# Output projections of both attentions from float32r high and low parts, on one Trainium2 core

## The chip, the core and the metric

The kernel runs on one core of a Trainium2 chip. The core's engines are TensorE (PE in the profile; its weight loads are PEld), VectorE (DVE), ScalarE (ACT), GpSimd (POOL) and SyncE (SP), which here only issues DMAs. Each engine works through its own list of instructions in order and waits on semaphores that others raise. The metric is device time in microseconds (us), as the median of several runs.

## The reference, cut to what matters

A perceiver block on 64 sequences of 64 tokens, width 256, 16 heads of 16: cross-attention to a context of 256 tokens per sequence, causal self-attention, and a feed-forward part with ternary weights and 8-bit activations. In float32:

```
x = x + xattn(layernorm(x), ctx, ctx)    # q, k, v = projections with bias; softmax; out @ Wo.T + bo
x = x + attn(layernorm(x))               # qkv = x @ w_qkv + b; causal; y @ w_out + b_out
x = x + ffn(layernorm(x))                # silu(gate) * up, then down, all quantized
```

The change touches the two products `out @ Wo.T` and `y @ w_out`.

## The kernel before, in words

The 4096 tokens are 32 tiles of 128 (two sequences each). There are three stages, one after the other over all tiles: cross-attention (about 14 to 560 us), self-attention (to about 790 us) and feed-forward. The order of each engine's instructions is written out by hand, in functions called from a `body` (cross-attention) or `body2` (self-attention); most tiles run in hardware loops (`Fori`), some are written out. In loops a wait whose count depends on the tile number takes instructions of its own (ISA, REGISTER_ALU); in written-out tiles it does not. On VectorE the cross-attention tiles 1 to 7 and 21 to 30 are in loops, 8 to 20 written out.

A cross-attention tile t has two halves s (one sequence each), called (t,0) and (t,1). TensorE's order in `body` is: keys k(t,1), transposes of the probabilities (t,0) in four groups, output projection of the tile before (`pe_out`, L361), values v(t,1) (`pe_v`, L299), transpose of the next tile's normalized rows (`pe_xt`, L264), scores (t,1) (L315), probabilities times values (t,0), queries of t+1, reciprocals r(t,0), keys (t+1,0), transposes (t,1), values (t+1,0), scores (t+1,0), and so on. The product with the values is `o`; VectorE multiplies it with the reciprocals (L428) and adds the two heads' parts into `oT` (L431).

The keys and values are already projected from float32r parts: `ch` is the context rounded to float32r by ScalarE, `cl` the rest, computed by GpSimd (L502), and three products (high by high, high by low, low by high) stand for the float32 one. The output projection is a plain float32 product of `oT` with `wo_sb`, two contraction steps, written by TensorE as four instructions.

`xt_ps`, the target of `pe_xt`, and `y_ps`, the target of `pe_out`, are the same 256 columns of one PSUM bank. For `pe_xt(t+1)` VectorE has to have written `xn` (L387): statistics (L375, L377), `vare` (L382), GpSimd's power (`rstd`, L493), then the normalization. VectorE's order there is: o(t-1,1), statistics of t+1, k(t,1) out of PSUM (L397), the reciprocal (L421), the copy of transposed group 0 (L414), xn, y of the tile before (L438), the copy of group 2, v(t,1).

In self-attention `pe_out2` (L725) does the same product per tile, behind the projection and r2 and ahead of `pe_v2` (L659). There GpSimd makes `rm` (L841), `kbd` (L833), `rstd`, the low part of the input (L826, `xl`, which shows as cl in the rows) and adds a bias to `x_all` (L848).

Of the kernel before, what the change touches and what calls it, by code (L numbers as in the profile page):

```python
# [26 lines left out]
P = 128  # L27
# [17 lines left out]
def block_kernel(nc, x, ctx_t, wq, bq, wk, bk, wv, bv, wo, bo, w_qkv, b_qk, b_v2, w_out, b_out,  # L45
# [8 lines left out]
    with ctx:  # L54
# [22 lines left out]
        wo_sb = sb("wo_sb", [P, KT, D])  # L77
        bq_sb = sb("bq_sb", [P, KT])
# [9 lines left out]
        wout_sb = sb("wout_sb", [P, KT, D])  # L88
        bout_sb = sb("bout_sb", [P, D])
# [29 lines left out]


# [8 lines left out]
        kbd4 = [sb(f"kbd4{s}", [P, KT, 4, P]) for s in range(2)]  # L129
# [19 lines left out]
        wd_b = wb_all[:, 8:12, :].rearrange("p a (c n) -> p (a c) n", c=2)  # L149
        w_abs = sb("w_abs", [P, 12])  # L150
# [80 lines left out]
        o_ev = sem("o_ev")  # L231
        y_mm = sem("y_mm")
# [190 lines left out]
        def dve_o(v, t, s):  # L423
            b = t * 2 + s
            v.wait_ge(pv_mm, b + 1)
            v.wait_ge(r_ev, b + 1)
            v.wait_ge(o_ev, b)
            nc.vector.tensor_tensor(o_prod[:], o_ps, r_sb[:], ALU.mult).then_inc(op_done, 1)  # L428
            v.wait_ge(op_done, b + 1)

            nc.vector.tensor_tensor(oT[:, :, s * L:(s + 1) * L], o_prod[:, :, 0, :],  # L431
                                    o_prod[:, :, 1, :], ALU.add).then_inc(o_ev, 1)
# [136 lines left out]
        def act_w2h(a, i):  # L569
            a.wait_ge(w2_in, 16 * len(SET2))  # L570
            nc.scalar.activation(w2h_p[:, i, :], wqkv_p[:, i, :], ACT.Copy).then_inc(w2h_split, 1)

        def pool_w2l(p, i):
            p.wait_ge(w2h_split, i + 1)
            nc.gpsimd.tensor_tensor(w2l_p[:, i, :], wqkv_p[:, i, :], w2h_p[:, i, :].bitcast(F32),
                                    ALU.subtract).then_inc(w2l_split, 1)
# [143 lines left out]
        def pe_out2(pe, t, turned=None):  # L720
            pe.wait_ge(o2_ev, t + 1)
            pe.wait_ge(y2_ev, t)
            pe.wait_ge(xh_done, t + 6 if turned is None else turned)
            for k in range(KT):
                last = nc.tensor.matmul(y2_ps, oT2[:, k, :], wout_sb[:, k, :],  # L725
                                        start=k == 0, stop=k == KT - 1)
            last.then_inc(y2_mm, 1)
# [23 lines left out]
        def dve_o2(v, t):  # L751
            v.wait_ge(pv2_mm, t + 1)
            v.wait_ge(r2_ev, t + 1)
            v.wait_ge(y2_mm, t)
            nc.vector.tensor_tensor(oT2[:], o2_ps, r2_sb, ALU.mult).then_inc(o2_ev, 1)
# [49 lines left out]

        def act_r2(a, t):
# [22 lines left out]
        def pool_kbd4(p, t, n, s, j):  # L829
            p.wait_ge(kk_ev, n * 2 + 2)  # L830
            if not isinstance(t, int) or t > 1:
# [4 lines left out]
                ALU.mult).then_inc(kbd4_pool, 1)  # L836

# [195 lines left out]
        with nc.Block() as block:  # L1033
# [27 lines left out]
            def _(pe):  # L1061
# [32 lines left out]
                body(0, True)  # L1094
                with pe.Fori(1, 8) as t:
                    body(t, False)
# [8 lines left out]
                pe_out(pe, t - 1, False)  # L1105
                pe_v(pe, t, 1)
                pe.wait_ge(k_ev, 2 * NT)
# [5 lines left out]
                pe.wait_ge(w2l_split, 3)  # L1113
# [16 lines left out]
                pe_out(pe, t, True)  # L1130
                pe_k2(pe, 1, 1)
                pe_xt2(pe, 4, x0_ps)
# [41 lines left out]
            def _(v):  # L1174
# [18 lines left out]
                def body(t, first, scale=False, piece=None):  # L1193
# [47 lines left out]
                dve_y(v, t - 1)  # L1241
                dve_stats(v, LN2, 1, at(1))
                dve_pt(v, t, 0, (2,))
                dve_v(v, t, 1)
                dve_xn(v, LN2, 1, at(1), xt2_mm)
# [52 lines left out]
            def _(a):  # L1298
# [11 lines left out]
                def body(t, pieces=None, w2=None):  # L1310
# [14 lines left out]
                body(0)  # L1325
# [4 lines left out]
                for i in range(3):  # L1330
                    body(22 + i, w2=i)
                with a.Fori(25, NT - 1) as t:
# [3 lines left out]
                t = NT - 1  # L1336
                act_pt(a, t, 0)
# [14 lines left out]
                act_xt2(a, 3, 1, 1, x0_ps)  # L1352
                act_k2(a, 1, 1)
# [3 lines left out]
                a.wait_ge(op_done, 2 * NT)  # L1357

                def body2(t):
                    act_v2(a, t, t % 2)  # L1360
                    act_pt2(a, t)
# [15 lines left out]
                act_xqt(a, 0)  # L1377
                act_scale_x(a, 1)

            @block.gpsimd  # L1380
            def _(p):
# [8 lines left out]
                def body(t, w2=None):  # L1390
                    pool_rstd(p, LN1, t + 1)
                    pool_rm(p, t, 0)
# [7 lines left out]
                body(0)  # L1400
                with p.Fori(1, 23) as t:
                    body(t)
                for i in range(3):
                    body(23 + i, i)
                with p.Fori(26, NT - 1) as t:
# [4 lines left out]
                pool_rstd(p, LN2, 0)  # L1410
                pool_rm(p, t, 0)
# [3 lines left out]
                pool_xl(p, 1, 0, 1)  # L1415
                pool_kbd4(p, 0, 0, 0, 0)
# [5 lines left out]
                pool_xl(p, 3, 1, 1)  # L1422
                for i in range(4):
# [7 lines left out]
                def body2(t):  # L1431
                    pool_rm2(p, t)
                    if t + 2 < NT:
# [12 lines left out]
                pool_fgu(p, 0, 0)  # L1446
                pool_rstd3(p, 1)
# [159 lines left out]
```

## Time and profile before

| | us |
|---|---|
| median of 3 runs | 950.61 (948.52 to 951.25) |
| the profiled execution | 948.79 |
| its span, first to last instruction | 947.0 |
| PE busy | 888.6 (94%) |
| DVE busy | 790.7 (83%) |
| ACT busy | 690.9 (73%) |
| POOL busy | 344.8 (36%) |

The busy time of matmuls counts their pipelined ends, so TensorE at 94% isn't at its peak; how long a step holds TensorE is read as the distance between the starts of two groups of its instructions. The granted TensorE clock is 0.991 of full speed over the span.

### The profile page before, as it was taken

The numbers are of one execution on the slowest core, as the hardware profiler recorded it, in microseconds if no ns is written. First come the engines' busy times: TensorE is split into PE (matmuls) and PEld (weight loads), VectorE is DVE, ScalarE is ACT, GpSimd is POOL, SyncE is SP. The second block draws the span as 40 slices with busy tenths as digits, with TensorE's granted clock in tenths as the row PEclk, the third lists the DMA queues.
The fourth block names the chain that finished last, engine by engine and source line by source line (L and its number), as shares of the span: only waits on it lengthen the run. The fifth ranks groups of instructions, "written<-read, shape, count | busy, mean of one in ns | idle before, by whom it ended". The sixth has DMA issues, their size and how long they took to land. (4 is left out here: it accounts for less than half of the span.)

```text
span 947.0 us, 29217 instructions
## 1 busy us (share of the span) xinstructions
PE 888.6 (94%) x9714; PEld 722.3 (76%) x9730; DVE 790.7 (83%) x1711; ACT 690.9 (73%) x1983; POOL 344.8 (36%) x487
## 2 busy tenths in 40 slices
PE   5899999999999999999999988999999987999997
PEld 4788888888888888888888876878787863555554
DVE  3788878888888888887788877988888876999997
ACT  3587776776777767777677665777777765988887
POOL 1322322223222232224322337767666632222221
PEclk9999999999999999999999999999999997999999
DMA  9111111111111111111111000000000000000001
GB/s 303 37 39 39 43 34 40 40 39 34 39 39 44 39 34 39 39 44 39 34 39 39 28 1 2 1 2 0 1 0 1 2 1 1 28 28 28 28 28 39
DMA packets 31618, 31.64 MB, mean 33 GB/s; under 512 B 3280, under 2 KB 30800, under 8 KB 31568
## 3 DMA queue, kind: packets, MB, share of 16 engines
q1 hardware_dynamic: 30720, 30.73, 10.5%
q8 instruction: 20, 0.33, 0.1%
q10 hardware_dynamic: 848, 0.33, 0.1%
q14 instruction: 30, 0.25, 0.1%
HBM read 26.86 MB, written 4.19 MB: 33 GB/s over the span
## 5 line engine op out<-in xcount | busy, mean ns | idle before, releaser
L485 ACT ACTIVATE probs<-psum,nmax 128x256 f32<-128x256 f32 x512 | 237.8, 488 | 89.6 <-DVE nmax L445 89.6
L445 DVE TENSOR_REDUCE nmax<-psum 128x2 f32<-128x512 f32 x256 | 159.0, 684 | 30.8 <-PE psum L315 30.8
L328 PE MATMUL psum<-id_sb,probs 128*128 128x128 f32 x1024 | 136.4, 277 | 14.3 <-ACT probs L485 14.1
L328 PEld LDWEIGHTS psum<-id_sb,probs 128*128 128x128 f32 x1024 | 111.8, 141 | 30.3 <-ACT probs L485 29.2
L493 POOL TENSOR_TENSOR rstd<-vare,minus_half 128x1 f32<-128x1 f32 x96 | 52.9, 551 | 182.2 <-DVE vare L382 179.7
L502 POOL TENSOR_TENSOR cl<-c_sb,ch 128x512 fp32r<-128x512 f32 x64 | 81.7, 1276 | 99.8 <-ACT ch L460 99.8
L485 ACT ACTIVATION_READ_ACCUMULATOR probs<-psum,nmax 128x1 f32 x512 | 112.7, 220 | 0.0
L466 ACT ACTIVATE probsT<-psum 128x512 f32<-128x512 f32 x160 | 91.0, 625 | 9.0 <-PE psum L328 8.9
L509 POOL TENSOR_TENSOR rm<-rinv,hm_sb 128x256 f32<-128x256 f32 x64 | 39.8, 622 | 127.7 <-DVE rinv L421 127.7
L315 PE MATMUL psum<-k_sb,qb 32*128 32x256 f32 x1024 | 78.4, 404 | 0.0
L1006 PE MATMUL psum<-wb_all,xqT 128*128 128x512 bf16 x240 | 66.2, 390 | 10.3 <-DVE probs L906 7.0
L351 PE MATMUL psum<-probsT,v_sb 128*32 128x128 f32 x2048 | 69.5, 276 | 0.0
L351 PEld LDWEIGHTS psum<-probsT,v_sb 128*32 128x32 f32 x2048 | 52.2, 110 | 21.4 <-issue 15.4
L392 DVE TENSOR_TENSOR v_sb<-psum,bv_sb 128x512 f32<-128x512 f32 x64 | 44.3, 691 | 24.0 <-PE psum L299 24.0
L414 DVE COPY probsT<-psum 128x512 f32<-128x512 f32 x96 | 62.8, 654 | 0.0
L833 POOL TENSOR_TENSOR kbd<-c_sb,qm_sb 128x1024 f32<-128x1024 f32 x32 | 60.6, 1894 | 2.9 <-ACT c_sb L783 2.9
L315 PEld LDWEIGHTS psum<-k_sb,qb 32*128 32x128 f32 x1024 | 51.1, 186 | 11.2 <-issue 5.9
L299 PE MATMUL psum<-wvh,ch 128*128 128x256 f32 x256 | 59.4, 313 | 0.0
L452 ACT ACTIVATE xnT<-psum 128x256 f32<-128x256 f32 x32 | 12.3, 384 | 62.6 <-PE psum L264 62.6
L284 PE MATMUL psum<-ch,wkh 128*128 128x256 f32 x256 | 56.6, 302 | 0.0
L1006 PEld LDWEIGHTS psum<-wb_all,xqT 128*128 128x128 bf16 x256 | 23.0, 99 | 42.1 <-DVE probs L906 20.5
L813 ACT ACTIVATE sc<-sc 128x1024 f32<-128x1024 f32 x32 | 33.9, 1060 | 27.8 <-DVE sc L738 27.8
(126 smaller groups left out, 2303.5 us busy)
## 6 DMA issues: line engine op xcount, KB each, us to landing
c_sb<-in_ctx_t SPq DMA_DIRECT2D x64, 256.0 KB, 2.7
x_sb<-in_x SPq DMA_DIRECT2D x32, 128.0 KB, 2.0
out<-y_sb SPq DMA_DIRECT2D x32, 128.0 KB, 1.7
w_all<-in_w_gate SPq DMA_DIRECT2D x1, 1024.0 KB, 7.9
w_all<-in_w_up SPq DMA_DIRECT2D x1, 1024.0 KB, 10.0
w_all<-in_w_down SPq DMA_DIRECT2D x1, 1024.0 KB, 12.5
wqkv_sb<-in_w_qkv SPq DMA_DIRECT2D x1, 768.0 KB, 6.3
wq_sb<-in_wq ACTq DMA_DIRECT2D x1, 256.0 KB, 3.9
```

Source lines behind the costliest of these rows:

```text
L284: last = nc.tensor.matmul(k_ps[:, m, :], w[:, k, cols], c[s][:, k, :], start=n + k == 0, stop=n == 2 and k == KT - 1)
L299: last = nc.tensor.matmul(v_ps[:, kh, :], c[s][:, k, keys], w[:, k, :], start=n + k == 0, stop=n == 2 and k == KT - 1)
L315: last = nc.tensor.matmul(sp[c][:, m * S:(m + 1) * S], qb[m][rows, s, :, :].rearrange("p h q -> p (h q)"), k_sb[rows, m, :], start=True, s ...
L328: last = nc.tensor.transpose(sp[g][:, c:c + P], probs[:, 2 * g + u, kh * P:(kh + 1) * P], id_sb[:])
L351: last = nc.tensor.matmul(op[32 * c:32 * c + 32, m * P:(m + 1) * P], v_sb[s][:, kh, 32 * j:32 * j + 32], probsT[:, 2 * c + m, kh, :], star ...
L414: nc.vector.tensor_copy(probsT[:, 2 * g:2 * g + 2, :, :].rearrange("p a b c -> p (a b c)"), sp[g]).then_inc(pt_dve, 1)
L445: nc.vector.tensor_reduce(nmax[:, 2 * g:2 * g + 2], sp[g].rearrange("p (u s) -> p u s", u=2), AX.X, ALU.max, negate=True).then_inc(max_don ...
L466: nc.scalar.activation(probsT[:, 2 * g:2 * g + 2, :, :].rearrange("p a b c -> p (a b c)"), sp[g], ACT.Copy).then_inc(pt_act, 1)
L485: nc.scalar.activation(probs[:, j, :], sp[g][:, u * S:(u + 1) * S], ACT.Exp, bias=nmax[:, j:j + 1], accum_out=rsum[:, j:j + 1]).then_inc(e ...
L502: nc.gpsimd.tensor_tensor(cl[s][:], c_sb[s][:], ch[s][:].bitcast(F32), ALU.subtract).then_inc(cl_done, 1)
L833: nc.gpsimd.tensor_tensor(kbd4[j][:], kT2[s][:, :, j * P:(j + 1) * P].unsqueeze(2).to_broadcast([P, KT, 4, P]), qm4_sb[:].unsqueeze(1).uns ...
L1006: last = nc.tensor.matmul(ps[n], xqT[:, k, :], w[:, k, n * 512:(n + 1) * 512], start=k == 0, stop=k == KT - 1)
```

## The change

Both output projections are made of three float32r products (six matmuls in place of the float32 pair). `woh`, `wol` (and `w2oh`, `w2ol`) are the parts of the weights, `oh`, `ol` those of `oT` or `oT2`: ScalarE rounds, GpSimd subtracts. In the cross-attention `pe_out` moves behind `pe_v(t,1)`, and since `xt_ps` and `y_ps` are one place, `pe_xt(t+1)` moves ahead of both. VectorE's xn moves ahead of the copy of group 0, and its y behind v. The two `kbd4` buffers now lie in `w_all`, which is free by then, and GpSimd waits for that once. The core of the diff:

```diff
         def pe_xt(pe, t):
             pe.wait_ge(xn_done, t + 1)
-            if not isinstance(t, int) or t > 1:
-                pe.wait_ge(y_ev, t - 1)
+            if not isinstance(t, int) or t > 2:
+                pe.wait_ge(y_ev, t - 2)
...
         def pe_q(pe, t):
             pe.wait_ge(xt_ev, t + 1)
+            if not isinstance(t, int) or t > 1:
+                pe.wait_ge(y_ev, t - 1)
...
-        def pe_out(pe, t, last_tile):
-            pe.wait_ge(o_ev, t * 2 + 2)
+        def pe_out(pe, t, last_tile, turned=None):
+            pe.wait_ge(ol_done, t + 1)
             pe.wait_ge(qb_done, t * 4 + (4 if last_tile else 8))
-            for k in range(KT):
-                last = nc.tensor.matmul(y_last if last_tile else y_ps, oT[:, k, :], wo_sb[:, k, :],
-                                        start=k == 0, stop=k == KT - 1)
+            pe.wait_ge(xt_ev, t + 3 if turned is None else turned)
+            to = y_last if last_tile else y_ps
+            for n, (o, w) in enumerate(((oh, woh), (oh, wol), (ol, woh))):
+                for k in range(KT):
+                    last = nc.tensor.matmul(to, o[:, k, :], w[:, k, :],
+                                            start=n + k == 0, stop=n == 2 and k == KT - 1)
...
+        def act_woh(a):
+            a.wait_ge(w1_in, 16 * len(SET1))
+            nc.scalar.activation(woh[:], wo_sb[:], ACT.Copy).then_inc(woh_split, 1)
+
+        def act_oh(a, t):
+            a.wait_ge(o_ev, t * 2 + 2)
+            a.wait_ge(y_mm, t)
+            nc.scalar.activation(oh[:], oT[:], ACT.Copy).then_inc(oh_done, 1)
...
+        def pool_wol(p):
+            p.wait_ge(woh_split, 1)
+            nc.gpsimd.tensor_tensor(wol[:], wo_sb[:], woh[:].bitcast(F32),
+                                    ALU.subtract).then_inc(wol_split, 1)
+
+        def pool_ol(p, t):
+            p.wait_ge(oh_done, t + 1)
+            nc.gpsimd.tensor_tensor(ol[:], oT[:], oh[:].bitcast(F32), ALU.subtract).then_inc(ol_done, 1)
...
         def pe_out2(pe, t, turned=None):
-            pe.wait_ge(o2_ev, t + 1)
+            pe.wait_ge(ol2_done, t + 1)
...
+        def act_oh2(a, t):
+            a.wait_ge(o2_ev, t + 1)
+            a.wait_ge(y2_mm, t)
+            nc.scalar.activation(oh[:], oT2[:], ACT.Copy).then_inc(oh2_done, 1)
...
                     pe_k(pe, t, 1)
                     pe_transpose(pe, t, 0)
+                    pe_xt(pe, t + 1)
+                    pe_v(pe, t, 1)
                     if not first:
                         pe_out(pe, t - 1, False)
-                    pe_v(pe, t, 1)
-                    pe_xt(pe, t + 1)
                     pe_scores(pe, t, 1)
...
                 body(0, True)
+                pe.wait_ge(wol_split, 1)
                 with pe.Fori(1, 8) as t:
...
-                pe_out(pe, t, True)
                 pe_k2(pe, 1, 1)
+                pe_out(pe, t, True, NT)
...
                     dve_inverse(v, t, 0)
-                    dve_pt(v, t, 0, (0,))
                     dve_xn(v, LN1, t + 1, x_sb[:], xt_mm)
-                    if not first:
-                        dve_y(v, t - 1)
-                    dve_pt(v, t, 0, (2,))
+                    dve_pt(v, t, 0, (0, 2))
...
                     dve_v(v, t, 1)
+                    if not first:
+                        dve_y(v, t - 1)
...
+                def body(t, pieces=None, w2=None, first=False):
+                    if not first:
+                        act_oh(a, t - 1)
                     act_pt(a, t, 0)
...
+                body(0, first=True)
+                act_woh(a)
...
                     act_v2(a, t, t % 2)
+                    if t > 0:
+                        act_oh2(a, t - 1)
                     act_pt2(a, t)
...
                 act_xqt(a, 0)
+                act_oh2(a, NT - 1)
                 act_scale_x(a, 1)
...
                     pool_rstd(p, LN1, t + 1)
+                    if not first:
+                        pool_ol(p, t - 1)
                     pool_rm(p, t, 0)
...
+                body(0, first=True)
+                pool_wol(p)
...
                     pool_rm2(p, t)
+                    if t > 0:
+                        pool_ol2(p, t - 1)
...
                 pool_rstd3(p, 0)
                 pool_fgu(p, 0, 0)
+                pool_ol2(p, NT - 1)
                 pool_rstd3(p, 1)
```

TensorE in a cross-attention loop tile, from the last group of transposes (`probs`) to the first scores (`k_sb,qb`). Before:

```order
L328 MATMUL psum<-id_sb,probs 128x128 x4
L358 ISA
L359 ISA
L361 MATMUL psum<-wo_sb,oT 128x256 x2
L299 MATMUL psum<-wvh,ch 128x256 x2
L299 MATMUL psum<-wvl,ch 128x256 x2
L299 MATMUL psum<-wvh,cl 128x256 x2
L299 MATMUL psum<-wvh,ch 128x256 x2
L299 MATMUL psum<-wvl,ch 128x256 x2
L299 MATMUL psum<-wvh,cl 128x256 x2
L260 REGISTER_ALU
L264 MATMUL psum<-id_sb,xn 128x128 x2
```

and of the changed kernel, in the same place:

```order
L341 MATMUL psum<-id_sb,probs 128x128 x4
L271 REGISTER_ALU
L273 REGISTER_ALU
L275 MATMUL psum<-id_sb,xn 128x128 x2
L312 MATMUL psum<-wvh,ch 128x256 x2
L312 MATMUL psum<-wvl,ch 128x256 x2
L312 MATMUL psum<-wvh,cl 128x256 x2
L312 MATMUL psum<-wvh,ch 128x256 x2
L312 MATMUL psum<-wvl,ch 128x256 x2
L312 MATMUL psum<-wvh,cl 128x256 x2
L372 ISA
L377 MATMUL psum<-woh,oh 128x256 x2
```

The transposes of xn moved from behind the values to directly behind the transposes of the probabilities, and the output projection (three pairs; the first is shown) from ahead of the values to behind them.

VectorE in the same loop, from k out of PSUM to v out of PSUM. Before:

```order
L397 TENSOR_TENSOR k_sb<-psum,bk_sb 128x512
L419 ISA
L421 RECIPROCAL rinv<-rsum 128x8
L413 ISA
L414 COPY probsT<-psum 128x512
L387 TENSOR_SCALAR xn<-x_sb,mv,rstd 128x256
L438 ISA
L438 TENSOR_TENSOR x_all<-psum,x_all 128x256
L413 REGISTER_ALU
L414 COPY probsT<-psum 128x512
L392 TENSOR_TENSOR v_sb<-psum,bv_sb 128x512
```

and of the changed kernel:

```order
L413 TENSOR_TENSOR k_sb<-psum,bk_sb 128x512
L435 ISA
L437 RECIPROCAL rinv<-rsum 128x8
L403 TENSOR_SCALAR xn<-x_sb,mv,rstd 128x256
L429 ISA
L430 COPY probsT<-psum 128x512
L429 REGISTER_ALU
L430 COPY probsT<-psum 128x512
L408 TENSOR_TENSOR v_sb<-psum,bv_sb 128x512
```

xn now follows the reciprocal at once, one copy earlier than before.

## Rows read from the trace of the kernel before

**Rows 1.** Busy time by stage: us, then PE, PEld, DVE, ACT, POOL, PEclk, DMA share, GB/s

```profile
30.00:560.00 530.00, 516.74 (x6019) 455.07 (x6020) 441.04 (x974) 382.14 (x1332) 161.72 (x189) 1.00 0.13 37
...
590.00:780.00 190.00, 187.17 (x2413) 151.22 (x2411) 167.08 (x305) 142.60 (x341) 120.30 (x134) 1.00 0.00 1
```

**Rows 2.** Timeline, loop tile, first half: start us, us, engine, line, what [idle before]

```profile
503.10 0.66 PE L328 MATMUL psum<-id_sb,probs 128*128 128x128 f32 x4 [0.26 <-ACT probs L485]
503.12 0.55 POOL L493 TENSOR_TENSOR rstd<-vare,minus_half 128x1 f32<-128x1 f32 x1 [4.70 <-DVE vare L382]
503.60 1.03 PE L361 MATMUL psum<-wo_sb,oT 128*128 128x256 f32 x4
503.60 0.19 DVE L421 RECIPROCAL rinv<-rsum 128x8 f32<-128x8 f32 x1
...
504.26 0.41 DVE L387 TENSOR_SCALAR xn<-x_sb,mv,rstd 128x256 f32<-128x256 f32 x1
504.27 0.59 PE L299 MATMUL psum<-wvh,ch 128*128 128x256 f32 x2
```

**Rows 3.** Timeline of PE in the same tile, from the scores (t,1) on

```profile
506.18 1.15 PE L315 MATMUL psum<-k_sb,qb 32*128 32x256 f32 x16
...
509.26 0.38 PE L338 MATMUL psum<-id_sb,rm 128*128 128x128 f32 x2
509.40 0.48 PE L284 MATMUL psum<-ch,wkh 128*128 128x256 f32 x2
...
512.57 0.48 PE L299 MATMUL psum<-wvh,ch 128*128 128x256 f32 x2
512.88 0.40 PE L299 MATMUL psum<-wvl,ch 128*128 128x256 f32 x2
...
513.82 0.39 PE L299 MATMUL psum<-wvh,cl 128*128 128x256 f32 x2
514.14 1.15 PE L315 MATMUL psum<-k_sb,qb 32*128 32x256 f32 x16
```

**Rows 4.** Timeline, a tile that VectorE has written out

```profile
315.34 0.55 POOL L493 TENSOR_TENSOR rstd<-vare,minus_half 128x1 f32<-128x1 f32 x1 [4.57 <-DVE vare L382]
...
315.99 1.03 PE L361 MATMUL psum<-wo_sb,oT 128*128 128x256 f32 x4
```

**Rows 5.** Timeline in the self-attention: xn beside a subtraction on GpSimd

```profile
665.43 0.73 POOL L826 TENSOR_TENSOR cl<-xnT,ch 128x256 fp32r<-128x256 f32 x1 [1.54 <-ACT ch L775]
665.49 0.82 DVE L387 TENSOR_SCALAR xn<-x_all,mv,rstd 128x256 f32<-128x256 f32 x1 [0.18 <-issue]
```

**Rows 6.** Timelines of DVE and of PE in tile 0

```profile
25.47 0.41 DVE L387 TENSOR_SCALAR xn<-x_sb,mv,rstd 128x256 f32<-128x256 f32 x1
...
25.93 0.69 PE L264 MATMUL psum<-id_sb,xn 128*128 128x128 f32 x2 [3.73 <-DVE xn L387]
26.55 2.09 PE L315 MATMUL psum<-k_sb,qb 32*128 32x256 f32 x16
```

**Rows 7.** Timelines of POOL and of PE in tile 1

```profile
35.75 1.27 POOL L502 TENSOR_TENSOR cl<-c_sb,ch 128x512 fp32r<-128x512 f32 x1 [1.33 <-ACT ch L460]
...
38.04 0.48 PE L284 MATMUL psum<-ch,wkh 128*128 128x256 f32 x2
...
42.28 1.03 PE L361 MATMUL psum<-wo_sb,oT 128*128 128x256 f32 x4
```

**Rows 8.** Timeline of a self-attention tile around the output projection

```profile
659.98 0.62 POOL L841 TENSOR_TENSOR rm<-rinv,ones 128x256 f32<-128x256 f32 x1
...
662.40 1.03 PE L725 MATMUL psum<-wout_sb,oT 128*128 128x256 f32 x4
...
663.08 0.59 PE L659 MATMUL psum<-w2h,ch 128*128 128x256 f32 x2
```

**Rows 9.** Timeline at the end of the self-attention

```profile
788.53 0.19 POOL L935 TENSOR_TENSOR vare<-mv,eps_col 128x1 f32<-128x1 f32 x1 [0.98 <-DVE mv L377]
...
788.80 0.38 ACT L963 ACTIVATE xqT<-psum 128x256 bf16<-128x256 f32 x1 [0.78 <-PE psum L993]
```

More of the change, by code:

```diff
@@ L77, in block_kernel @@
         wo_sb = sb("wo_sb", [P, KT, D])
+        woh, wol = sb("woh", [P, KT, D], F32R), sb("wol", [P, KT, D], F32R)
         bq_sb = sb("bq_sb", [P, KT])
@@ L126, in block_kernel @@
         xh, xl = ch, cl
-        kbd4 = [sb(f"kbd4{s}", [P, KT, 4, P]) for s in range(2)]
         v2b = [sb(f"v2b{s}", [P, D]) for s in range(2)]
@@ L149, in block_kernel @@
         wd_b = wb_all[:, 8:12, :].rearrange("p a (c n) -> p (a c) n", c=2)
+        kbd4 = [w_all[:, 2 * i:2 * i + 2, :].rearrange("p k (h t) -> p k h t", h=4) for i in range(2)]
         w_abs = sb("w_abs", [P, 12])
@@ L231, in block_kernel @@
         o_ev = sem("o_ev")
+        woh_split = sem("woh_split")
+        wol_split = sem("wol_split")
+        oh_done = sem("oh_done")
+        ol_done = sem("ol_done")
+        oh2_done = sem("oh2_done")
+        ol2_done = sem("ol2_done")
         y_mm = sem("y_mm")
@@ L570, in act_w2h @@
             a.wait_ge(w2_in, 16 * len(SET2))
-            nc.scalar.activation(w2h_p[:, i, :], wqkv_p[:, i, :], ACT.Copy).then_inc(w2h_split, 1)
+            if i < 3:
+                nc.scalar.activation(w2h_p[:, i, :], wqkv_p[:, i, :], ACT.Copy).then_inc(w2h_split, 1)
+            else:
+                nc.scalar.activation(w2oh[:], wout_sb[:], ACT.Copy).then_inc(w2h_split, 1)
         def pool_w2l(p, i):
             p.wait_ge(w2h_split, i + 1)
-            nc.gpsimd.tensor_tensor(w2l_p[:, i, :], wqkv_p[:, i, :], w2h_p[:, i, :].bitcast(F32),
-                                    ALU.subtract).then_inc(w2l_split, 1)
+            if i < 3:
+                nc.gpsimd.tensor_tensor(w2l_p[:, i, :], wqkv_p[:, i, :], w2h_p[:, i, :].bitcast(F32),
+                                        ALU.subtract).then_inc(w2l_split, 1)
+            else:
+                nc.gpsimd.tensor_tensor(w2ol[:], wout_sb[:], w2oh[:].bitcast(F32),
+                                        ALU.subtract).then_inc(w2l_split, 1)
         b_set = sem("b_set")
@@ L720, in pe_out2 @@
         def pe_out2(pe, t, turned=None):
-            pe.wait_ge(o2_ev, t + 1)
+            pe.wait_ge(ol2_done, t + 1)
             pe.wait_ge(y2_ev, t)
             pe.wait_ge(xh_done, t + 6 if turned is None else turned)
-            for k in range(KT):
-                last = nc.tensor.matmul(y2_ps, oT2[:, k, :], wout_sb[:, k, :],
-                                        start=k == 0, stop=k == KT - 1)
+            for n, (o, w) in enumerate(((oh, w2oh), (oh, w2ol), (ol, w2oh))):
+                for k in range(KT):
+                    last = nc.tensor.matmul(y2_ps, o[:, k, :], w[:, k, :],
+                                            start=n + k == 0, stop=n == 2 and k == KT - 1)
             last.then_inc(y2_mm, 1)
@@ L836, in pool_kbd4, with pool_ol2 @@
                 ALU.mult).then_inc(kbd4_pool, 1)
+        def pool_ol2(p, t):
+            p.wait_ge(oh2_done, t + 1)
+            nc.gpsimd.tensor_tensor(ol[:], oT2[:], oh[:].bitcast(F32), ALU.subtract)\
+              .then_inc(ol2_done, 1)
         def pool_rm2(p, t):
@@ L1244, in _ @@
                 dve_v(v, t, 1)
+                dve_y(v, t - 1)
                 dve_xn(v, LN2, 1, at(1), xt2_mm)
@@ L1329, in _ @@
                     body(t)
-                for i in range(3):
+                for i in range(4):
                     body(22 + i, w2=i)
-                with a.Fori(25, NT - 1) as t:
+                with a.Fori(26, NT - 1) as t:
                     body(t)
                 t = NT - 1
+                act_oh(a, t - 1)
                 act_pt(a, t, 0)
@@ L1352, in _ @@
                 act_xt2(a, 3, 1, 1, x0_ps)
+                act_oh(a, t)
                 act_k2(a, 1, 1)
@@ L1388, in _, with body @@
                 pool_c(p, 0, 1)
-                def body(t, w2=None):
+                def body(t, w2=None, first=False):
                     pool_rstd(p, LN1, t + 1)
+                    if not first:
+                        pool_ol(p, t - 1)
                     pool_rm(p, t, 0)
@@ L1398, in body @@
                         pool_w2l(p, w2)
-                body(0)
+                body(0, first=True)
+                pool_wol(p)
                 with p.Fori(1, 23) as t:
                     body(t)
-                for i in range(3):
+                for i in range(4):
                     body(23 + i, i)
-                with p.Fori(26, NT - 1) as t:
+                with p.Fori(27, NT - 1) as t:
                     body(t)
@@ L1410, in _ @@
                 pool_rstd(p, LN2, 0)
+                pool_ol(p, t - 1)
                 pool_rm(p, t, 0)
@@ L1415, in _ @@
                 pool_xl(p, 1, 0, 1)
+                p.wait_ge(wq_step, 36)
                 pool_kbd4(p, 0, 0, 0, 0)
@@ L1422, in _ @@
                 pool_xl(p, 3, 1, 1)
+                pool_ol(p, t)
                 for i in range(4):
```

13 lines of the change are left out of this document (7 added, 6 removed).

## The prediction

> **What bounds the kernel now.** I read the busy time by stage first. TensorE works 516.7 of 530 us in the cross-attention and 187.2 of 190 in the self-attention, and VectorE, the next, 441.0 and 167.1 [rows 1]. So both stages that the change touches go at TensorE's pace, and what the change does to the time is what it does to the distance between TensorE's groups: its own work, and the waits it is given. Then I read one cross-attention tile in order of time, and in it the waits. The tile repeats about every 17.0 us. In its first half TensorE waits for ScalarE's exponentials: the last four transposes of (t,0) begin at 503.10, behind a wait that the last exponential ended, and what follows begins at 503.60 [rows 2]. From there on TensorE runs without a wait of size through the output projection, values, the transpose of xn and the scores at 506.18, and on to the scores of the next tile at 514.14 [rows 2, 3]. So a delay between 503.60 and 506.18 moves everything behind it by as much, and a gain there counts in full. Nothing further on gives it back: the next wait, for exponentials, hangs on the scores of that same next tile.
>
> **TensorE's own work.** Before, the stretch from 503.60 to 506.18 is 2.58 us: projection, values, xn's transpose. After, the order is xn's transpose, values, projection. Two transposes ahead of a float32r group hold TensorE 0.14 (509.26 to 509.40). Values behind transposes and up to the scores take 1.57 (512.57 to 514.14). A pair of float32r matmuls takes (513.82 - 512.88) / 4 = 0.235, three pairs 0.70 [rows 3]. The sum is 2.41, so the six matmuls save 0.17 us a tile against the float32 product. This has no cover and no doubt of size: bounds 0.10 (the extra wait ahead of the projection costs its instruction) and 0.22.
>
> **The wait for xn in the cross-attention.** Before, xn's transpose stood behind 2.1 us of other TensorE work, and xn, begun at 504.26 and done at 504.67, was never waited for in the steady tiles. Now TensorE asks for it at 503.60. What has to be done until then: GpSimd's rstd runs from 503.12 to 503.67, and the reciprocal begins at 503.60 [rows 2]. Moving xn ahead of the copy lets it begin at about 503.72, no earlier, since rstd is late. It takes 0.41, and TensorE begins 0.05 after it, as in tile 0 (25.47 + 0.41, then 25.93) [rows 6]. That makes 504.18, a new wait of 0.58, 0.41 net of the saving. Everything queued on TensorE stands behind this wait: values, projection, scores.
>
> There is more. On GpSimd `ol` of the tile before is now directly behind rstd. Its input oh is ready: ScalarE is through with the exponentials just before 503.10, which they released, and needs about 0.38 for 128x256 [rows 9], so `ol` can begin at 503.65, just ahead of xn. In the self-attention the trace has this pair: a GpSimd subtraction of the same form, begun at 665.43, and xn at 665.49. There xn took 0.82 in place of 0.41 and ended 0.15 after the subtraction did [rows 5]. By that row `ol` lasts 0.73, to 504.38, xn ends at 504.53, and TensorE begins at 504.58: a wait of 0.98, net +0.81 a tile. Bounds for the net cost: +0.41 (no hindrance) and +0.81. I take the upper one, since the one row of the same pair in the same sequence of starts has it.
>
> The Trainium skill (SBUF — State Buffer, "Who interferes with whom") says that a VectorE instruction that uses both its ports and a GpSimd instruction shut each other out for their whole length, and that the one issued first wins. The trace agrees in rows 5; by this rule the cost is the upper bound, and without it the lower one.
>
> In tiles 8 to 20, where VectorE is written out, rstd ends at 315.89 while TensorE arrives at 315.99 [rows 4]. By the same steps: `ol` to 316.61, xn to 316.76, TensorE at 316.81, a wait of 0.82 and net +0.65; without the hindrance 316.40, net +0.24. Sixteen tiles of the loops (2 to 7, 21 to 30) and 13 written out: 16 x 0.81 + 13 x 0.65 = 21.4 us. Without the hindrance 16 x 0.41 + 13 x 0.24 = 9.7. Tile 31 has no such transpose in front: -0.2.
>
> **What lies beside other work.** `oh` on ScalarE delays only the copies of transposed groups; the later of these waits for the transposes begun at 503.10 anyway, and the scores that need it come 2.4 us after. ScalarE's copy of the transposed xn comes more than a us earlier than before, and the context's with it. `rm` on GpSimd moves back by 0.7, and its transpose on TensorE stands at 509.26 [rows 3]. `ol` is done two us before the projection asks. VectorE's y now runs between v and the maxima, in the time of the scores, and the queries, which wait for it, stand behind scores and values. kbd4's wait is for work long done. If this cover were gone, each would cost its own length, 0.4 to 0.7 a tile.
>
> **Tile 0.** TensorE stood idle 3.73 us for xn, with the values (0,1) done in front. Now the values are behind xn. xn comes 0.5 earlier (the copy goes behind it), the values add 1.57 - 0.1: +1.0 [rows 3, 6].
>
> **Tile 1.** TensorE waits for `wol` ahead of k(1,1). ScalarE makes `woh` only after the exponentials of (1,0), which end just before 41.8 (TensorE's last transposes and then the projection at 42.28 hang on them, 0.50 apart as in rows 2). `woh` is twice the 0.38 row, less the fixed part, about 0.6 [rows 9]; the subtraction of 128x512 is 1.27. So k(1,1) begins at about 43.65, not at 38.04 [rows 7]. k and the transposes then run without waits, 3.17 us (509.40 to 512.57, rows 3), to 46.8, where 42.28 stood: +4.5. After the idle 3.73 us in tile 0 the scores took 2.09 rather than 1.15 [rows 3, 6]; an idle time of 5.6 should bring the same slower stretch, 1.2 for that. Together +5.7, bounds 4.5 and 6.5.
>
> **Self-attention.** Output projection and values stand in the same order as before, TensorE has work all the time, and the same float32 group (0.68 from 662.40 to 663.08) is replaced [rows 8]: -0.17 x 31 = -5.3. The new chain is o2, oh2, ol2, projection. In the tile shown `rm` ends at 660.60, `ol2` with 0.73 at 661.3, and the projection is asked for at 662.40, 1.1 later. GpSimd is busy 120 of 190 us and gets 31 x 0.73 = 23 more [rows 1, 5, 8]; it has room. Bounds: -5.3, and +12.7 if the hindrance of rows 5 came in each tile here (31 x 0.41).
>
> **The end of the self-attention.** `ol2` of the last tile stands on GpSimd ahead of the second rstd of the feed-forward. `oh2` comes behind ScalarE's copy at 788.80 (0.38 each), to 789.5, `ol2` to 790.3, and the small `vare` that began at 788.53 begins there: +1.8 [rows 9]. The engines meet behind this chain, so it counts in full.
>
> **The sum**, against the profiled execution of 948.79: 1.0 + 5.7 + 21.4 - 0.2 - 5.3 + 1.8 = +24.4, that is 973.2. The median of the runs is 1.8 above the profiled one, and the same run-to-run spread will hold, so I say 974.
>
> **Rivals.**
> 1. xn isn't hindered by `ol` (or wins the race, since the two starts are only about 0.07 apart). For it: xn beside `rm` in the steady tiles took its plain 0.41. Against: `rm` was about to end there. Then 1.0 + 5.7 + 9.7 - 0.2 - 5.3 + 1.8 = +12.7: 961.5.
> 2. Not slower: xn is there when TensorE asks. The place is 503.60 and its like; the price falls from 21.4 to -0.17 x 29 = -4.9. Sum 1.0 + 5.7 - 4.9 - 0.2 - 5.3 + 1.8 = -1.9: 946.9. It decides at a mean wait below about 0.06 us a tile. Against it is that rstd alone ends at 503.67. For it only that rstd or the reciprocal could come earlier if VectorE's k found its input sooner, which nothing in the change does. If the wait in tile 1 were hidden also, 941.
> 3. The self-attention turns from TensorE to VectorE: GpSimd's extra subtraction hinders VectorE, which has only 23 us of slack there. On top of my case: +12.7 in place of -5.3, 991. For it: rows 5. Against: that pair took its toll once in the tiles I read, and `ol2` runs while VectorE reads PSUM.
>
> **Chances.** Mine 0.62, rival 1 0.18, rival 3 0.08, rival 2 0.07, and 0.05 for times between mine and rival 1 with the hindrance in part of the tiles. Mine alone spans 968 to 980. Leaving out most of rivals 2 and 3, the range is 959 to 982. This measurement tells 0.3% from no change. Rival 2 gives 0.05 for the same and 0.03 for faster; all else is slower, 0.92.
>
> **What will show it.** In the changed profile: TensorE idle ahead of xn's transpose (`xn`, 128x128) in 29 tiles, mean near 0.9, released by VectorE's xn; xn at about 0.8 with `ol` on GpSimd beside it; a wait of 5.6 us for `wol` near 38 us; the values directly behind the transpose and the projection in about 0.70; the self-attention shorter by 5 us with no wait at its projection; rstd at the end 1.8 later. I am wrong if TensorE's wait at xn is under 0.4 in the mean, if xn stays at 0.41, or if the self-attention grows.

## The result, and the profile after

| | before | after |
|---|---|---|
| median of the runs | 950.66 (948.52 to 951.25, 4) | 982.92 (982.62 to 983.87, 4) |
| ratio, 95% interval | | 1.0349 (1.0331 to 1.0366) |
| the profiled execution | 948.79 | 982.8 |
| its span | 947.0 | 980.9 |
| PE busy | 888.6 (94%) | 889.5 (91%) |
| POOL busy | 344.8 (36%) | 388.2 (40%) |

The changed kernel is 3.5% slower. TensorE's busy time is about what it was; what it gained is distance between its groups. To place the 33.9 us of the spans I cut both traces at the first matmul of named groups:

| stretch | before | after | difference | predicted |
|---|---|---|---|---|
| to the scores (1,0): tile 0 | 35.76 | 36.40 | +0.6 | +1.0 |
| to the scores (2,0): tile 1 | 17.14 | 23.92 | +6.8 | +5.7 |
| to the scores (31,0): tiles 2 to 30 | 495.27 | 523.65 | +28.4 | +21.4 |
| to the first transposes of self-attention | 32.95 | 33.03 | +0.1 | -0.2 |
| 31 self-attention tiles | 200.45 | 196.07 | -4.4 | -5.3 |
| the rest | 165.43 | 167.84 | +2.4 | +1.8 |
| sum | 947.0 | 980.9 | +33.9 | +24.4 |

Two of these rows move between executions of the same instructions by more than their difference. The first took 36.40 here and 38.25 when the changed kernel was profiled again (run 8), and 34.24 in run 4, whose cross-attention is that of before. The fourth took 33.03 here and 31.71 in run 8. The other rows repeated within 0.8 us, but for the half-clock tiles told of below. So the +0.6 and the +0.1 say nothing about the change.

The shares of the stages, in the form of [rows 1] (us, then PE, PEld, DVE, ACT, POOL, PEclk, DMA share, GB/s), the cross-attention and the self-attention of after:

```profile
60.00:550.00 490.00, 457.29 (x5346) 400.73 (x5344) 398.64 (x852) 340.62 (x1189) 161.26 (x194) 0.99 0.13 36
...
617.00:807.00 190.00, 187.49 (x2542) 154.20 (x2538) 169.82 (x311) 155.20 (x377) 145.54 (x170) 1.00 0.00 1
```

In the cross-attention TensorE is busy 457 of 490 us where it was 517 of 530; in the self-attention it is full as before, and GpSimd has more to do (146 of 190, it was 120). A steady tile of after, the stretch that answers to [rows 2]: start us, us, engine, line, what, and in brackets the idle time of the engine before it.

```profile
517.79 0.46 ACT L486 ACTIVATE oh<-oT 128x256 fp32r<-128x256 f32 x1
...
518.00 0.66 PE L341 MATMUL psum<-id_sb,probs 128*128 128x128 f32 x4 [0.26 <-ACT probs L511]
518.01 0.55 POOL L519 TENSOR_TENSOR rstd<-vare,minus_half 128x1 f32<-128x1 f32 x1 [3.48 <-DVE vare L398]
518.50 0.19 DVE L437 RECIPROCAL rinv<-rsum 128x8 f32<-128x8 f32 x1
518.53 0.72 POOL L538 TENSOR_TENSOR ol<-oT,oh 128x256 fp32r<-128x256 f32 x1
518.61 0.80 DVE L403 TENSOR_SCALAR xn<-x_sb,mv,rstd 128x256 f32<-128x256 f32 x1
519.53 0.43 PE L275 MATMUL psum<-id_sb,xn 128*128 128x128 f32 x2 [0.88 <-DVE xn L403]
519.77 0.47 PE L312 MATMUL psum<-wvh,ch 128*128 128x256 f32 x2
...
521.25 0.40 PE L377 MATMUL psum<-woh,oh 128*128 128x256 f32 x2
521.49 0.40 PE L377 MATMUL psum<-wol,oh 128*128 128x256 f32 x2
521.72 0.39 PE L377 MATMUL psum<-woh,ol 128*128 128x256 f32 x2
522.04 1.15 PE L328 MATMUL psum<-k_sb,qb 32*128 32x256 f32 x16
```

`ol` begins 0.08 ahead of xn, xn takes 0.80 in place of the 0.41 of [rows 2], and TensorE stands until 519.53. The bracket says 0.88, but that is counted from the modelled end of the transposes (518.00 + 0.66). TensorE would have gone on 0.50 after their start, as before (503.10 to 503.60), so the wait that counts is 519.53 - 518.50 = 1.03. From there to the scores it is 2.51.

The waits of PE by what ended them (us, times, the longest), whole kernel, after:

```profile
PE psum L275 <- DVE xn L403: 28.3, 30, 4.8
PE psum L297 <- POOL wol L533: 5.8, 1, 5.8
```

The first row had one entry before, in tile 0 (3.7 us, [rows 6]). The second is tile 1, which answers to [rows 7] (PE, then POOL, then PE):

```profile
38.48 0.44 PE L351 MATMUL psum<-id_sb,rm 128*128 128x128 f32 x2
...
42.97 1.26 POOL L533 TENSOR_TENSOR wol<-wo_sb,woh 128x512 fp32r<-128x512 f32 x1 [5.29 <-ACT woh L481]
...
44.67 0.79 PE L297 MATMUL psum<-ch,wkh 128*128 128x256 f32 x2 [5.75 <-POOL wol L533]
47.40 2.67 PE L341 MATMUL psum<-id_sb,probs 128*128 128x128 f32 x16
49.91 0.38 PE L275 MATMUL psum<-id_sb,xn 128*128 128x128 f32 x2
```

And two tiles that no step of the prediction has. Windows of after, in and just ahead of tile 3:

```profile
83.40:86.40 3.00, 1.78 (x12) 1.30 (x13) 2.88 (x9) 2.29 (x8) 1.99 (x4) 1.00 0.00 0
86.50:89.90 3.40, 3.40 (x18) 3.28 (x16) 1.19 (x2) 1.42 (x4) 1.76 (x2) 0.50 0.12 39
```

In the second TensorE's granted clock is 0.50, its lower level of 1.2 GHz, for about 3.4 us, behind a stretch of 3.00 us in which it was busy 1.78. The same comes at 124.0 to 127.5, in tile 5. These tiles take 19.62 and 19.67 us, their neighbours 18.0.

### The profile page after: what moved, and what is told of

The parts are those of the page before. It is cut to its first block and busy times, and to the rows that moved or that the text cites. A ratio compares the mean times of both kernels' runs of the same rounds, so it can differ in the third digit from the quotient of the medians.

```text
span 980.9 us, 29760 instructions
## 1 busy us (share of the span) xinstructions
PE 889.5 (91%) x9842; PEld 725.8 (74%) x9858; DVE 803.2 (82%) x1711; ACT 710.0 (72%) x2049; POOL 388.2 (40%) x553
## 5 line engine op out<-in xcount | busy, mean ns | idle before, releaser
L881 POOL TENSOR_TENSOR w_all<-c_sb,qm_sb 128x1024 f32<-128x1024 f32 x32 | 60.6, 1894 | 4.2 <-ACT c_sb L826 4.2
L312 PE MATMUL psum<-wvh,ch 128*128 128x256 f32 x256 | 57.0, 304 | 0.0
L312 PE MATMUL psum<-wvl,ch 128*128 128x256 f32 x256 | 52.2, 286 | 0.0
```

What stands on the lines that cost most here:

```text
L312: last = nc.tensor.matmul(v_ps[:, kh, :], c[s][:, k, keys], w[:, k, :], start=n + k == 0, stop=n == 2 and k == KT - 1)
L881: nc.gpsimd.tensor_tensor(kbd4[j][:], kT2[s][:, :, j * P:(j + 1) * P].unsqueeze(2).to_broadcast([P, KT, 4, P]), qm4_sb[:].unsqueeze(1).uns ...
```

## The experiments

The theory after the result: (1) the loss in tiles 2 to 30 is TensorE's wait for xn, and a good half of it is that `ol` on GpSimd lengthens xn; (2) the six matmuls themselves save; (3) tile 1 is the wait for `wol`; (4) what the order costs is separate from what the arithmetic costs, and the order is forced only by `xt_ps` and `y_ps` being one place. The rival: the float32r projection or its extra instructions on ScalarE and GpSimd slow the tile by themselves.

**1. `ol` held back until xn is written.**

```diff
                     if not first:
+                        p.wait_ge(xn_done, t + 2)
                         pool_ol(p, t - 1)
```

> The changed kernel, with GpSimd's subtraction ol in the cross-attention made to wait until xn of the same tile is written. Theory (the subtraction holds xn up): xn falls from 0.80 to about 0.41 us, TensorE's wait for it from 0.88 to about 0.50 in the loop tiles (0.71 to 0.33 in the written-out ones), 29 x 0.38 = 11 us less, and up to 3 more if the two tiles with a slow TensorE clock go with it: 969 to 972. Rival (xn is slow because of its new place behind the reciprocal, whatever GpSimd does): xn stays at 0.8 and the time at 983.

Measured: 970.31 (969.95 to 971.82), ratio 1.0197 (1.0173 to 1.0220) to the kernel before, 12.6 us under the changed kernel. The same stretch of a tile:

```profile
507.58 0.66 PE L341 MATMUL psum<-id_sb,probs 128*128 128x128 f32 x4 [0.26 <-ACT probs L511]
...
508.07 0.19 DVE L437 RECIPROCAL rinv<-rsum 128x8 f32<-128x8 f32 x1
508.18 0.41 DVE L403 TENSOR_SCALAR xn<-x_sb,mv,rstd 128x256 f32<-128x256 f32 x1
508.67 0.73 POOL L538 TENSOR_TENSOR ol<-oT,oh 128x256 fp32r<-128x256 f32 x1 [0.53 <-DVE xn L403]
508.72 0.43 PE L275 MATMUL psum<-id_sb,xn 128*128 128x128 f32 x2 [0.48 <-DVE xn L403]
```

and over all tiles, the xn instructions (shortest/median/longest in ns), first of after, then of this run:

```profile
L403 DVE TENSOR_SCALAR xn<-x_sb,mv,rstd x32: 363/801/809, 4.9 to 572.5; 128x256 f32<-128x256 f32 x32
```

```profile
L403 DVE TENSOR_SCALAR xn<-x_sb,mv,rstd x32: 366/410/415, 4.8 to 560.9; 128x256 f32<-128x256 f32 x32
```

xn lasts 0.41 at its median and PE's waits for it sum to 16.4 us in place of 28.3. The edit moves only `ol` and what stands behind it on GpSimd, and run 3, which has no `ol`, has xn at 0.41 too, so the lengthening of xn by `ol` is shown. The tiles 2 to 30 take 509.47 us, 14.2 less than in the changed kernel. Of these 14.2, 3.1 are the tiles 3 and 5, since this run has no tile at half the clock; the other 11.1 are 0.38 a tile. So `ol` beside xn is 11.1 of the 25.3 us that are not the clock's: under half of them, where the theory had a good half. The spans of the two profiles differ by less, 11.3, mainly since tiles 0 and 1 took 2.2 more in this one.

The rule that the prediction leaned on (the Trainium skill, SBUF — State Buffer, "Who interferes with whom") is borne out with one limit. In the kernel before, `rm` on GpSimd was already running when xn began at 504.26 [rows 2], and xn kept its 0.41:

```profile
503.87 0.62 POOL L509 TENSOR_TENSOR rm<-rinv,hm_sb 128x256 f32<-128x256 f32 x1 [0.20 <-DVE rinv L421]
```

xn ended 0.18 behind `rm` there, and 0.14 to 0.16 behind `ol` in the tiles 2 to 30 of the changed kernel. An estimate from these rows: a GpSimd instruction that is already running costs xn time only if it has more than about 0.25 left (0.41 less 0.16).

**2. `woh` and `wol` made early.** ScalarE rounds in tile 0 and GpSimd subtracts ahead of its body of tile 0.

```diff
                     act_pt(a, t, 0)
+                    if first:
+                        act_woh(a)
                     act_xt(a, t + 1)
...
-                body(0, first=True)
                 pool_wol(p)
+                body(0, first=True)
```

> The changed kernel, with the weights' parts woh and wol made in tile 0, where ScalarE and GpSimd are idle, in place of behind it. Theory (TensorE's 5.75 us in tile 1 is the wait for wol alone, and the slow clock behind it follows from the idle time): tile 1 shrinks from 23.9 to about 18.0 us, 5.9 us less in all, 977. Rival (tile 1 waits next for the exponentials, and the cost of the idle time was hidden by them): 2 us less, 981.

Measured: 977.21 (976.09 to 977.34), ratio 1.0267 (1.0242 to 1.0291), 5.7 us under the changed kernel. Tile 1 takes 18.21 us where it took 23.92, and PE has no wait for `wol` left. What tile 1 is still longer than before, 1.1 us, is about what every loop tile of this order loses. Of the tiles 2 to 30 one took 19.58, tile 26, again at half the clock:

```profile
490.00:494.00 4.00, 2.68 (x21) 1.97 (x19) 3.14 (x10) 3.87 (x14) 1.41 (x3) 1.00 0.06 20
494.50:497.90 3.40, 3.40 (x18) 3.40 (x18) 1.38 (x3) 0.90 (x2) 1.94 (x2) 0.50 0.13 39
```

**3. The new order with the old arithmetic.** The cross-attention's projection stays a float32 product, in its new place; `oh`, `ol`, `woh` and `wol` are not made there. The self-attention is as changed.

```diff
         def pe_out(pe, t, last_tile, turned=None):
-            pe.wait_ge(ol_done, t + 1)
+            pe.wait_ge(o_ev, t * 2 + 2)
...
-            for n, (o, w) in enumerate(((oh, woh), (oh, wol), (ol, woh))):
-                for k in range(KT):
-                    last = nc.tensor.matmul(to, o[:, k, :], w[:, k, :],
-                                            start=n + k == 0, stop=n == 2 and k == KT - 1)
+            for k in range(KT):
+                last = nc.tensor.matmul(to, oT[:, k, :], wo_sb[:, k, :],
+                                        start=k == 0, stop=k == KT - 1)
```

> The changed order of the cross-attention with the float32 projection of before: no oh, ol, woh, wol there; the self-attention keeps the float32r parts. It tells the order from the arithmetic. Theory (TensorE waits for xn because of the order, and ol adds 0.39 to it): xn about 0.41, TensorE's wait 0.50 in the loop tiles and 0.33 in the others, nothing in tile 1; against before 16 x 0.6 + 13 x 0.45 = +15.5, tile 0 +0.6, self-attention and its end -2: 965. Rival (the wait does not depend on ol): 29 x 0.38 more, 976.

Measured: 970.36 (968.39 to 971.57), ratio 1.0198 (1.017 to 1.0226). Its tile has no `ol`, and xn is short:

```profile
503.56 0.66 PE L341 MATMUL psum<-id_sb,probs 128*128 128x128 f32 x4 [0.26 <-ACT probs L509]
...
504.16 0.41 DVE L402 TENSOR_SCALAR xn<-x_sb,mv,rstd 128x256 f32<-128x256 f32 x1
...
504.32 0.72 POOL L542 TENSOR_TENSOR rm<-rinv,hm_sb 128x256 f32<-128x256 f32 x1 [0.20 <-DVE rinv L436]
...
504.70 0.43 PE L275 MATMUL psum<-id_sb,xn 128*128 128x128 f32 x2 [0.49 <-DVE xn L402]
504.93 0.47 PE L312 MATMUL psum<-wvh,ch 128*128 128x256 f32 x2
```

The order alone, with nothing of the float32r projection in the cross-attention, costs 0.72 us a loop tile (17.85, written out 17.59), 19.0 us over the tiles 2 to 30 (514.29). Run 1, with the same wait and the float32r product, takes 17.70: the product saves 0.15 us of it, and its extra instructions cost the tile nothing once `ol` keeps off xn. That speaks against the rival, but for the part of it that goes through xn. The time lies between what the theory and the rival gave (965 and 976), since I had worked out 0.60 a tile. The missing 0.10 is in the last two rows: after a wait, the transposes hold TensorE 0.23 to 0.24 before the values begin, where the 0.14 of [rows 3] is from an unbroken stream. (The other such place in an unbroken tile, the transposes of (t,1) ahead of its keys, takes 0.19.)

**4. Float32r in the self-attention alone.** The cross-attention is that of before, line for line.

> The kernel before with the float32r parts in the self-attention alone. Theory: the stretch of 31 self-attention tiles is 4.4 us shorter as in the changed kernel, and its end 2.4 longer: 948.7, 2 us less than before. Rival (the 4.4 are an effect of the other stage, for instance of when the context's transfers end): no difference, 950.7.

Measured: 948.87 (946.34 to 952.26), ratio 0.9981 (0.9962 to 1.0001), beside a kernel before at 951.51. In the profiled execution the 31 tiles take 197.24 us rather than 200.45, and the rest 168.24 rather than 165.43: 3.2 us are gained, not the expected 4.4, and 2.8 go again at the end. The median is 2.6 under that of before as forecast, but the interval just holds no change, so the gain of the whole is not shown. The shorter tiles are there with the cross-attention of before, which speaks against the rival.

**5. y out of the place of xn's transpose.** Float32r in both, `y_ps` in the free half of the bank of `o`, so that xn's transpose can stand behind the values and the projection. TensorE's order is k, transposes, v, projection, xn's transpose, scores. The product with the values waits for y's evacuation. `woh` and `wol` are early, as in run 2, and VectorE's xn is behind its first copy again.

```diff
-        y_ps = mp[:, 0:D]
+        y_ps = op[:, D:2 * D]
...
             pe.wait_ge(o_ev, b)
+            if s == 0 and (not isinstance(t, int) or t > 0):
+                pe.wait_ge(y_ev, t)
...
                     pe_transpose(pe, t, 0)
-                    pe_xt(pe, t + 1)
                     pe_v(pe, t, 1)
                     if not first:
                         pe_out(pe, t - 1, False)
+                    pe_xt(pe, t + 1)
                     pe_scores(pe, t, 1)
```

> The float32r parts in both stages, with y of every tile in a PSUM bank of its own kind (the free half of the bank of o), so that the projection can stand behind the values and the transpose of xn still behind both; xn back behind the first copy; woh and wol made in tile 0. Theory (all the loss is the wait for xn, ol beside it and the wait for wol; the matmuls themselves save 0.15 us a tile in both stages): no wait ahead of xn's transpose, tiles of about 16.95 us against 17.1, 951.5 - 4.6 - 4.4 + 2.4 = 944.9. Rival (oh and ol delay something else as well, for instance the copies of the probabilities or r): tiles stay at 17.1 or above, 949 or more.

Measured: 943.37 (942.59 to 944.19), ratio 0.9920 (0.9899 to 0.9940): 39.6 us under the changed kernel with the same arithmetic, and faster than before. Its tile:

```profile
500.14 0.66 PE L337 MATMUL psum<-id_sb,probs 128*128 128x128 f32 x4 [0.25 <-ACT probs L508]
...
500.55 0.48 PE L308 MATMUL psum<-wvh,ch 128*128 128x256 f32 x2
...
500.67 0.75 POOL L535 TENSOR_TENSOR ol<-oT,oh 128x256 fp32r<-128x256 f32 x1
...
501.30 0.85 DVE L400 TENSOR_SCALAR xn<-x_sb,mv,rstd 128x256 f32<-128x256 f32 x1
...
502.74 0.38 PE L273 MATMUL psum<-id_sb,xn 128*128 128x128 f32 x2
503.05 1.15 PE L324 MATMUL psum<-k_sb,qb 32*128 32x256 f32 x16
```

xn takes 0.85 in this tile too. This time it is `rm` that holds it up: `ol` is nearly done when xn begins, and xn ends 0.15 behind this instruction, which by the recorded starts began 0.07 after xn:

```profile
501.37 0.63 POOL L541 TENSOR_TENSOR rm<-rinv,hm_sb 128x256 f32<-128x256 f32 x1
```

xn is that long in the 17 tiles in VectorE's loops (1 to 7, 21 to 30), where it begins 0.06 to 0.08 ahead of `rm`; in the written-out tiles, where it is 0.10 to 0.12 ahead, it takes 0.40. So which of the two is held up hangs here on a few hundredths of a microsecond, and not simply on the recorded order of their starts. It ends at 502.15 and is asked for 0.6 later, so the lengthening costs nothing. PE's waits for xn are one, in tile 0:

```profile
PE psum L273 <- DVE xn L400: 4.3, 1, 4.3
```

A loop tile takes 16.96 us (written out 16.85), 0.17 under the 17.13 of before, which is the saving that the prediction gave the six matmuls.

**6. The same, with the last `ol2` behind the second rstd of the feed-forward.**

```diff
                 pool_fgu(p, 0, 0)
-                pool_ol2(p, NT - 1)
                 pool_rstd3(p, 1)
+                pool_ol2(p, NT - 1)
```

> As e5_y_apart, and at the end of the self-attention the last ol2 stands behind the second rstd of the feed-forward on GpSimd. Theory (ol2 ahead of that rstd costs its wait, 1.7 us, directly on the chain): 1.7 less than e5_y_apart, 943.2. Rival (the projection of the last tile, now later, ends the stage instead): same as e5_y_apart.

Measured: 942.17 (940.05 to 944.20), ratio 0.9910 (0.9889 to 0.9931): the lowest median here, though not told apart from run 5. The rstd came back, but the rest shrank by 0.5 us (167.85 to 167.35) and not by 1.7, so the rival was nearer; 1.9 of the 2.3 us between the spans of the two profiles lie in the first row of the table above, where the two kernels are the same.

Now the projection of the last tile itself is what comes late, and VectorE waits for it (POOL, PE, DVE):

```profile
779.92 0.81 POOL L885 TENSOR_TENSOR ol<-oT,oh 128x256 fp32r<-128x256 f32 x1 [0.21 <-ACT oh L849]
...
780.79 0.80 PE L765 MATMUL psum<-w2oh,oh 128*128 128x256 f32 x2 [1.67 <-POOL ol L885]
...
782.48 0.42 DVE L800 TENSOR_TENSOR x_all<-psum,x_all 128x256 f32<-128x256 f32 x1 [1.48 <-PE psum L765]
```

At that place `oh2`, `ol2` and the projection are one chain, and turning its order with rstd only changes which end of it is late.

**7. The changed kernel with runs 1 and 2 and the edit of run 6,** keeping the order.

> The changed order with three edits at once: ol behind xn, woh and wol in tile 0, the last ol2 behind rstd. Theory: the savings add up, 970.3 - 5.9 - 1.7 = 962.7, and what is left over before is the wait of 0.48 or 0.32 us for xn in each of 29 tiles and the transposes that no longer follow other work without a break. Rival (they overlap): 966.

Measured: 963.88 (963.06 to 964.78), ratio 1.0133 (1.0106 to 1.0160), tiles of 17.70 and 17.43. The repairs add up to within 1.2 us, and with them this order, with the cheaper product in it, is still 1.3% slower than before.

**8 and 9. The changed kernel and run 3 once more,** without an edit, to see whether the tiles at half the clock stay in their place.

> The changed kernel unchanged, for a second profile: are the two tiles (3 and 5) with a TensorE clock at half speed part of the kernel, or of that execution? Theory (they come from where TensorE's idle time of 0.9 falls, and differ from one execution to the next): some tiles of 19.6 us again, perhaps others, one to four of them. Rival (something fixed in tiles 3 and 5): exactly the same two.

> The changed order with the float32 projection, for a second profile, with TensorE's wait of 0.49 a tile. Theory (a shorter wait does not bring the clock down): no tile between 2 and 30 over 18.5 us. Rival (chance): one or more.

Measured: 982.79, with one such tile, tile 7 (19.57 us), and tile 1 at 24.64; and 968.11 with none, no tile above 18.2. So they are no property of a tile: in three executions of kernels with 0.7 to 0.9 us of idle time ahead of xn's transpose there were four (3 and 5, 26, 7), in four executions with at most 0.5 there (runs 1, 3, 7, 9) none. Nor is half the clock something of the changed order alone. Every profile here has it also in tile 0 and for 10 us or more at the end of the self-attention (from about 786 to 796 in the kernel before), and the 13 runs of the kernel before that stand beside runs 1 to 4 go from 947.43 us at a mean granted clock of 0.993 to 953.02 at 0.987.

## Why the prediction was wrong

The direction and the places were right. The size was 9.5 us short of the spans' difference (33.9 against 24.4), and the time, 982.92, lies 9 us above the forecast and 0.9 above the upper end of its range.

The step that failed is the price of the tiles 2 to 30. The prediction put them at +21.4 us; they took +28.4, which is 7.0 of the 9.5. Two things were wrong in it. The term for the wait was too small in each tile: 25.3 us were measured where 21.4 stood. And the clock, a term put at nothing in these tiles, took 3.1. The rest of the miss is smaller: +1.1 in tile 1, +0.9 in the self-attention, +0.6 at the end, and -0.1 in the two rows that don't repeat. The 1.8 us by which the median of the runs lay above the profiled execution before, and of which 0.8 went into the forecast of 974, was 0.1 after.

**The wait for xn: right in mechanism, short in size.** The price was bounded between no hindrance and that of [rows 5], and the upper end taken. It was the right end: `ol` begins 0.06 to 0.08 ahead in all of the 29 tiles, and xn takes 0.80 (run 1 shows the link). But what I called the upper bound, +0.81 a tile, was none. A loop tile went from 17.13 to 18.09 and a written-out one from 17.03 to 17.81. So the 28.4 us of tiles 2 to 30 are, to within 0.2, 16 x 0.96 + 13 x 0.78 = 25.5, where I had 16 x 0.81 + 13 x 0.65 = 21.4, and the 3.1 of the two tiles at half the clock. The 0.15 that a loop tile lost beyond the forecast has two parts.

- The step "two transposes ahead of a float32r group hold TensorE 0.14" took its price from an unbroken stream, for a place where my own next step put a wait. Measured there: 0.24 (519.53 to 519.77). The block to the scores is 2.51 and not 2.41. So of "the six matmuls save 0.17, this has no cover and no doubt of size", 0.07 is left in the stalled tiles, under its lower bound of 0.10. The arithmetic was priced right (0.15 between runs 3 and 1, 0.17 in run 5 against before); the place it was put in was not.
- xn came 0.05 later than I had it (519.53 - 518.50 = 1.03, predicted 0.98).

**The clock.** [rows 6] had shown me a slower stretch behind a long idle, and I priced it for tile 1 alone. That a tile could meet it at idle times of under 1 us, in a stream with TensorE 93% busy, was in no row. It is 3.1 us in the profiled execution. That the stretches follow from the longer waits is suggested by the tally under runs 8 and 9, four such tiles against none, and not shown; seven executions are few for an event this rare. Nor is it what took the time out of the range: run 8, with one such tile, took 982.79.

**Tile 0: +0.6, predicted +1.0, and not tested.** xn hangs there on the arrival of the rows `x_sb`, for which VectorE stood idle 5.54 us in the profile after and 5.38 in that before. The prediction didn't name this wait. Run 8 has 4.24 at the same place, and its tile 0 ends 1.9 us later all the same, so the step can't be read at this spread.

**Tile 1: +6.8, predicted +5.7.** k(1,1) began at 44.67, where I had 43.65. Of that 0.64 is the shift of tile 0, and nearly all the rest lies behind `wol`: it ended at 44.23, and TensorE began 0.44 later, with a loop to enter in between. Then the slow stretch covered keys and transposes, 5.24 us to xn's transpose at 49.91, where I had 3.17 and 1.2. Run 2 shows that 5.7 of the 6.8 hung on `wol`. The other 1.1 is what this order costs a tile in which `wol` is there in time, so the two prices don't add.

**Self-attention: -4.4, predicted -5.3.** No wait at the projection, as said; a tile saves 0.14 rather than 0.17. The three pairs in place, of after, answering to [rows 8]:

```profile
644.35 0.38 PE L743 MATMUL psum<-id_sb,rm 128*128 128x128 f32 x2
644.48 0.48 PE L768 MATMUL psum<-w2oh,oh 128*128 128x256 f32 x2
644.80 0.40 PE L768 MATMUL psum<-w2ol,oh 128*128 128x256 f32 x2
```

**The end: +2.4, predicted +1.8.** The chain through `oh2` and `ol2` is there, answering to [rows 9]:

```profile
815.85 0.50 PE L768 MATMUL psum<-w2oh,oh 128*128 128x256 f32 x2 [1.02 <-POOL ol L888]
...
821.67 0.41 ACT L852 ACTIVATE oh<-oT 128x256 fp32r<-128x256 f32 x1
822.16 0.72 POOL L888 TENSOR_TENSOR ol<-oT,oh 128x256 fp32r<-128x256 f32 x1 [2.01 <-ACT oh L852]
822.84 0.19 POOL L988 TENSOR_TENSOR vare<-mv,eps_col 128x1 f32<-128x1 f32 x1
```

From the first to the second xn of the feed-forward it is 4.87 us rather than 3.16, that is 1.7 of the predicted 1.8. The tile before it has a wait of 1.02 for its own `ol` as well, which I didn't look for.

**The rivals.** The first (xn not hindered) was made real by run 1 and came out at 970.3, not the 961.5 that it was given: the same undersized steps, 0.57 a loop tile in place of 0.41, and 0.41 written out in place of 0.24. The second (xn there in time) doesn't hold in this order, and in run 5, by another order, gave 943.4. The third (self-attention turns to VectorE) is out: that stage got shorter. The chances don't add up by 0.01: the second rival has 0.07 in the list, and 0.08 as "same" or "faster".

**What stays open.** Whether the longer waits are the cause of the half clock in tiles of the stream. And why the first float32r pair behind a broken stream of transposes comes 0.10 later: in the unbroken stream the weight load of the transposes (PEld) begins 0.11 ahead of them (509.15 and 509.26, the kernel before), and behind the wait the two begin together (519.53). The size fits, but no run tests it.

## What to carry to other kernels

When a cheaper product needs another place in the order, price the place apart from the product: here the product saves 4 to 5 us in each attention (the self-attention gives 2.4 of them back at its end), and between the changed kernel and run 5, which differ in the place and in tile 1's 5.7 us, lie 39.6. Ask first what forces the order; it was one PSUM tile used for two things, and moving one of them, with `woh` and `wol` made early, turned 3.5% slower into 0.8% faster. And where a step puts a wait into a stream, take the durations behind it from rows behind a wait, not from an unbroken stream, and leave room above the sum for the clock.

## What the runs showed of the hardware

- A float32 VectorE `tensor_scalar` of 128x256 (xn) took 0.80 us in place of 0.41 in all 29 tiles in which a GpSimd subtraction of the same size had begun 0.06 to 0.08 ahead of it, and 0.41 where it had GpSimd's time to itself (run 1). It ended 0.14 to 0.18 behind the GpSimd instruction, and with only 0.23 of `rm` left (the kernel before) it kept its 0.41.
- Where xn began 0.12 to 0.16 ahead of `rm` (run 3), it kept its 0.41 and `rm` took 0.72 to 0.77 in place of 0.62. Where it began 0.06 to 0.08 ahead of `rm`, with `ol` just ending (run 5), it took 0.83 to 0.85 and `rm` its 0.62.
- Six float32r matmuls of 128x256 took 0.15 to 0.17 us less than the float32 product of the same size (runs 3 and 1; run 5 and the kernel before).
- Two 128x128 transposes ahead of a float32r group held TensorE 0.14 or 0.19 us in an unbroken stream, and 0.23 at the median of the 31 places of the changed order, 30 of them behind a wait.
- The granted TensorE clock fell to 0.50 for about 3.4 us in a stream with idle times of no more than about a microsecond: in tiles 3 and 5, in tile 7 of a second execution of the same kernel, and in tile 26 of run 2.
